# A fused chain of convolutions and Newton inverses on one core: Newton steps as split fp32r products, convolution groups set between them

## The reference

```python
x = x + conv3x3(gn(x), weights) + bias            # A, zero padding
x = x + newton_inverse(gn(x), num_iters=5)        # B
x = x + circular_conv3x3(gn(x), weight)           # C, written as an FFT in the reference
x = x + conv3x3(gn(x), K)                         # D, last row and column of the convolution masked to zero
# gn: 8 groups of 2 channels, mean and variance over the group's 2 x 128 x 128 values
def newton_inverse(W, num_iters):
    scale = max_column_abs_sum(W).max_over_columns * max_row_abs_sum(W).max_over_rows
    X = W.T / scale
    for _ in range(num_iters):
        X = X @ (2 * I - W @ X)
    return X
```

## Time and profile before

| | |
|---|---|
| median of three runs | 698.35 us |
| profiled execution, its own time | 701.13 us |
| its span | 699.5 us |
| TensorE busy (matmuls) | 623.8 us, 89% |
| VectorE busy | 448.1 us, 64% |
| ScalarE busy | 348.9 us, 50% |
| GpSimd busy | 120.7 us, 17% |
| matmuls of V / R / the three convolutions | 168.9 / 137.4 / 303.6 us |
| first Newton step, last Newton product's end | 64.7 us, 641 us |

### The profile page before, as it was taken

The page is one execution under the profiler, slowest core; times in us unless marked ns, Lnnn a source line. Parts: engine busy times, 40 slices in busy tenths (PEclk is TensorE's granted clock), DMA queues, the critical chain, the costliest instruction groups (busy, mean ns, idle before and its releaser), DMA issues.

```text
span 699.5 us, 13159 instructions
## 1 busy us (share of the span) xinstructions
PE 623.8 (89%) x4200; PEld 533.8 (76%) x4200; DVE 448.1 (64%) x1454; ACT 348.9 (50%) x617; POOL 120.7 (17%) x235
## 2 busy tenths in 40 slices
PE   0596894999999999899989999899999999989756
PEld 0365894899879897698869897698879897888544
DVE  3868238766885857766876657856785648356560
ACT  0252552655457265454557374554567265546432
POOL 5024022120213021120212002120210021000202
PEclk9998997999999999999999999999999999999888
DMA  5131043252226314252235314262134214400432
GB/s 153 49 93 42 28 66 114 61 138 58 92 79 146 94 37 126 79 150 60 70 91 128 108 32 133 79 154 62 63 96 99 68 39 131 112 31 32 128 99 60
DMA packets 82837, 60.85 MB, mean 87 GB/s; under 512 B 8238, under 2 KB 75982, under 8 KB 81870
## 3 DMA queue, kind: packets, MB, share of 16 engines
q1 hardware_dynamic: 78558, 54.80, 28.8%
q0 software_dynamic: 4224, 5.43, 3.2%
HBM read 23.46 MB, written 16.91 MB: 58 GB/s over the span
## 4 chain that ended last, share of the span: by engine, by line
PE 69%; DVE 10%; DMA 7%; SPq 6%; issue 5%; ACT 2%; DVEq 0%; POOL 0%; ACTq 0%
PE conv_ps L612 31%; PE V_ps L763 18%; PE R_ps L753 16%; DMA win_C<-rows_dram 4%; SPq L315 3%; DVE x L959 2%; PE R_ps L702 2%; DMA rows_dram<-x 2%; DVE d_A L500 2%; SPq L282 1%; SPq L268 1%; PE V_ps L709 1%; DVE sums L902 1%; DMA x<-out_C 1%; ACT d_C L528 1%
## 5 line engine op out<-in xcount | busy, mean ns | idle before, releaser
L763 PE MATMUL V_ps<-V,R 128*128 128x128 f32 x1280 | 168.9, 276 | 0.0
L763 PEld LDWEIGHTS V_ps<-V,R 128*128 128x128 f32 x1280 | 156.0, 193 | 0.1
L753 PE MATMUL R_ps<-R 128*128 128x128 f32 x1024 | 137.4, 278 | 6.6 <-DVE R L939 6.6
L753 PEld LDWEIGHTS R_ps<-R 128*128 128x128 f32 x1024 | 125.9, 194 | 7.2 <-DVE R L939 7.2
L612 PE MATMUL conv_ps<-d_C,w_C 128*96 128x512 f32 (+1 forms) x486 | 115.7, 393 | 16.4 <-DVE d_C L500 6.4
L612 PEld LDWEIGHTS conv_ps<-d_C,w_C 128*96 128x96 f32 x486 | 76.0, 167 | 48.3 <-DVE d_C L500 11.2
L612 PE MATMUL conv_ps<-d_A,w_D 128*96 128x512 f32 (+1 forms) x432 | 99.6, 386 | 5.5 <-DVE w_D L493 3.9
L830 ACT ACTIVATE R<-R_ps 128x512 f32<-128x512 f32 x128 | 76.0, 594 | 43.0 <-PE R_ps L753 42.3
L832 ACT ACTIVATE V<-V_ps 128x512 f32<-128x512 f32 x128 | 76.3, 596 | 35.6 <-PE V_ps L763 35.6
L612 PE MATMUL conv_ps<-d_A,w_A 128*96 128x512 f32 (+1 forms) x378 | 88.3, 389 | 4.0 <-DVE d_A L500 4.0
L612 PEld LDWEIGHTS conv_ps<-d_A,w_D 128*96 128x96 f32 x432 | 66.8, 164 | 31.1 <-DVE w_D L493 4.0
(11 more groups left out here) (170 smaller groups left out, 644.7 us busy)
## 6 DMA issues: line engine op xcount, KB each, us to landing
win_C<-rows_dram SPq DMA_DIRECT2D x40, 256.0 KB, 4.0
rows_dram<-x SPq DMA_DIRECT2D x32, 256.0 KB
y<-out_D SPq DMA_DIRECT2D x160, 48.0 KB
win_D<-out_C SPq DMA_DIRECT2D x7, 1056.0 KB, 6.8
x<-out_A SPq DMA_DIRECT2D x139, 48.0 KB
win_A<-x SPq DMA_DIRECT2D x84, 64.0 KB
win_A<-x POOLq DMA_DIRECT2D x56, 64.0 KB, 2.8
win_D<-out_C SPq DMA_DIRECT2D x14, 160.0 KB, 5.9
```

Of the source, the lines that this page charges most:

```text
L753: ins = pe.matmul(R_ps[s][:, m, :], Rk[:, m, :], Rk[:, m, :], start=True, stop=True)
L763: ins = pe.matmul(V_ps[s][:, m, :], Rk[:, m, :], V[ch][:, m, :], start=False, stop=True, skip_group_check=True)
```

## The change

The steps are written anew. For each chunk PSUM holds [F | V] side by side, 256 columns a matrix. F starts as -N N^T / s (times a power of two), V as N^T / s with a minus sign; both accumulate over all steps in PSUM, which is never restarted. Between steps ScalarE writes the high part of [F | V] as fp32r, VectorE the low part, and the step multiplies [F | V] by F as high x high, high x low, low x high, 12 fp32r matmuls of 256 columns for four matrices. The last step is plain fp32 and of V alone. A cycle is 24 slots q, strand q % 2, position j = (q // 2) % 6 (0 the start, 1 to 4 split steps, 5 the last), round q // 12. Behind each slot but every fourth stands one convolution group: D of image i - 2 in slots 0 to 7, C of image i - 1 in 8 to 15, A of image i + 2 in 16 to 23. Transposes for the norms and the scale of image i + 1 are made in cycle i.

```diff
+        def pe_slot(pe, b, q):
+            s, r, j = place(q)
+            ch = 2 * r + s
+            if j == 0:
+                pe.wait_ge(s_DS, at(NCHK, b, ch + 1))
+                wait(pe, s_x2, at(NCHK, b, ch - 1 if r else s - 1))
+                for m in range(NMAT):
+                    pe.matmul(z[s][:, m, 128:256], DS[:, c, :], ident, start=m % 2 == 0, stop=True,
+                              is_transpose=True, skip_group_check=True)
+                for m in range(NMAT):
+                    ins = pe.matmul(z[s][:, m, 0:128], DN[:, c, :], DS[:, c, :], start=False, stop=True,
+                                    skip_group_check=True)
+            elif j < STEPS:
+                pe.wait_ge(s_zl[s], at(per_zh, b, (STEPS - 1) * r + j))
+                for m in range(NMAT):
+                    pe.matmul(z[s][:, m, :], zh[s][:, m, 0:128], zh[s][:, m, :], start=False, ...)
+                    pe.matmul(z[s][:, m, :], zh[s][:, m, 0:128], zl[s][:, m, :], start=False, ...)
+                    ins = pe.matmul(z[s][:, m, :], zl[s][:, m, 0:128], zh[s][:, m, :], start=False, ...)
+            else:
+                pe.wait_ge(s_z4[s], at(ROUNDS, b, r + 1))
+                for m in range(NMAT):
+                    ins = pe.matmul(z[s][:, m, 128:256], z4[s][:, m, 0:128], z4[s][:, m, 128:256], ...)
+            ins.then_inc(s_z[s], 1)
...
+        def act_slot(act, b, q):
+            if j == STEPS:
+                return
+            act.wait_ge(s_z[s], at(per_z, b, n_z(r, j)))
+            if j < STEPS - 1:
+                act.activation(zh[s][:, :, :], z[s][:, :, :], ACT.Copy, scale=ROOT[j]).then_inc(s_zh[s], 1)
+            else:
+                act.activation(z4[s][:, :, :], z[s][:, :, :], ACT.Copy, scale=ROOT[j]).then_inc(s_z4[s], 1)
...
+        def dve_slot(dve, b, q):
+            if j < STEPS - 1:
+                dve.wait_ge(s_zh[s], at(per_zh, b, (STEPS - 1) * r + j + 1))
+                dve.scalar_tensor_tensor(zl[s][:, :, :], z[s][:, :, :], ROOT[j], zh[s][:, :, :].bitcast(f32),
+                                         ALU.mult, ALU.subtract).then_inc(s_zl[s], 1)
+            elif j == STEPS:
+                dve_x2(dve, b, 2 * r + s, s, r)
```

TensorE's and VectorE's order around the rows of the next image (cut; each engine's slot stands first or last as shown):

```diff
+        def pe_cycle(pe, i, has_D, has_C, has_A, nxt, load):
+            for q in range(SLOTS):
+                if has_C and q == 3:
+                    row_mean_C(pe, i - 1)
...
+                if nxt and q == 8:
+                    row_mean_B(pe, i + 1)
...
+                pe_slot(pe, i, q)
+                pe_filler(pe, i, q, has_D, has_C, has_A)
...
+        def dve_cycle(dve, i, has_D, has_C, has_A, nxt, load):
+            for q in range(SLOTS):
+                dve_slot(dve, i, q)
+                if has_C and q == 1:
+                    row_stats_1(dve, x2, stC, sC_bn, 1)
...
+                if nxt and q == 5:
+                    dve.wait_ge(s_x1, x1_moved(i + 2))
+                    row_stats_1(dve, x1, stB, sB_bn, 0)
+                if has_C and q == 6:
+                    low_parts(dve, cC, i - 1, 0)
+                if nxt and q == 6:
+                    row_stats_1(dve, x1, stB, sB_bn, 1)
+                if nxt and q == 7:
+                    link_B = dve_rows_B_mean(dve, i + 1)
+                if has_C and q == 7:
+                    low_parts(dve, cC, i - 1, 1)
+                    low_parts(dve, cC, i - 1, 2)
```

SyncE's order. The copy of x1 to x2 is now a DMA, of the whole tensor:

```diff
+        def keep_x1(sp, b):
+            if is_int(b, 0):
+                sp.wait_ge(s_x1, x1_moved(1))
+                sp.wait_ge(s_x1_pool, 16 * n_x1_pool)
+            else:
+                sp.wait_ge(sC_bn, at(2, b, -1))
+            sp.dma_start(x2[:, :, :], x1[:, :, :]).then_inc(s_keep, 16)
...
+        def sp_cycle(sp, i, has_D, has_C, has_A, nxt, load):
+            if has_C:
+                for g in range(NG):
+                    load_x2(sp, i - 1, g)
+            keep_x1(sp, i)
+            if nxt:
+                sp.wait_ge(s_keep, at(16, i, 16))
+                sp.wait_ge(s_DN, at(NCHK, i, NCHK))
+                for g in range(NG):
+                    rows_from_windows(sp, i + 1, g)
+            if has_D:
+                store_y(sp, i - 2)
+            store_x2(sp, i, 0)
+            store_x2(sp, i, 1)
+            if has_C:
+                windows_from_windows(sp, i - 1)
+            if load:
+                for g in range(NG):
+                    load_x(sp, i + 3, g)
+            store_x2(sp, i, 2)
+            store_x2(sp, i, 3)
+            store_x2_edges(sp, i)
```

The low parts of A and D (all but the first two images' A and the last image's D) go to GpSimd, for which ScalarE subtracts the mean from the windows in place in a second activation. GpSimd also forms DS, the scaled DN:

```diff
+        def low_parts_pool(pool, c, b, g):
+            pool.wait_ge(c.s_dh, at(NG, b, g + 1))
+            pool.tensor_tensor(c.d[:, 1, k0:k0 + kn, 1:W + 1], c.win[:, k0:k0 + kn, :],
+                               c.d[:, 0, k0:k0 + kn, 1:W + 1].bitcast(f32), ALU.subtract).then_inc(c.s_dl, 1)
...
+            if low_by_pool(c, b):
+                ins = act.activation(c.win[:, k0:k0 + kn, :], c.win[:, k0:k0 + kn, :], ACT.Identity,
+                                     bias=col(c, NEG))
...
+        def pool_DS(pool, b, ch):
+            if ch == 0:
+                pool.wait_ge(s_sc, at(1, b, 1))
+            pool.tensor_tensor(DS[:, cs, :], DN[:, cs, :], scl[:, 1, cs].unsqueeze(2).broadcast_to([128, NMAT, 128]),
+                               ALU.mult).then_inc(s_DS, 1)
```

More of the change, by code:

```diff
@@ L84, in wait @@
     eng.wait_ge(sem, value)
+KAPPA = [2.0 ** (k - 1) for k in range(STEPS)]
+ROOT = [k ** 0.5 for k in KAPPA]
+SEGS = STEPS + 1
+SLOTS = 2 * ROUNDS * SEGS
 def build(nc, x, w0, b0, w2, w3, consts, y, rows_dram):
@@ L269, in load_x, with rows_from_windows @@
                               x[bass.ds(b, 1), :, lo:hi, :].rearrange("b c h w -> (b h) c w"))\
-                    .then_inc(by_sp if g in SP_X else by_pool, 16)
-        def rows_from_windows(eng, b, g, done=s_x1, first=0):
-            if g == first:
-                wait(eng, s_keep, at(1, b))
-                wait(eng, s_x2, at(NCHK, b - 1, 2))
+                    .then_inc(done, 16)
+        def rows_from_windows(eng, b, g, done=s_x1):
             eng.wait_ge(cA.s_out, at(NG, b, g + 1))
             k0, kn = SPLIT_G[g]
-            out = (cA1 if isinstance(b, int) and b == 1 else cA).out
+            out = (cA1 if is_int(b, 1) else cA).out
             for k in range(k0, k0 + kn):
@@ L696, in pe_gram, with place @@
-        def pe_gram(pe, b, ch):
-            s = ch % 2
-            if ch >= 2:
-                pe.wait_ge(s_R, at(per_R, b, n_R(0, STEPS - 2, s)))
-            for m in range(NMAT):
-                ins = pe.matmul(R_ps[s][:, m, :], DN[:, NMAT * ch + m, :], DN[:, NMAT * ch + m, :],
-                                start=True, stop=True)
-            ins.then_inc(s_Gr, 1)
-        def pe_transposes(pe, out, ch):
+        def place(q):
+            return q % 2, q // (2 * SEGS), (q // 2) % SEGS
@@ L708, in pe_transposes, with pe_norm_T @@
+        def pe_norm_T(pe, b, ch, out=None):
+            pe.wait_ge(s_DN, at(NCHK, b, ch + 1))
+            if out is None:
+                out = spare_ps
+                wait(pe, s_Ta, at(NCHK, b, ch))
             for m in range(NMAT):
@@ new lines, in pe_norm_spread, with pe_filler @@
+        def pe_norm_spread(pe, b):
+            pe.wait_ge(s_dg, at(1, b, 1))
+            pe.matmul(misc_ps[:, M_NB:M_NB + 2 * C], ones_all[0:2 * C, :], diag[:, :],
+                      start=True, stop=True).then_inc(s_nB, 1)
+        def pe_filler(pe, i, q, has_D, has_C, has_A):
+            part, g = filler(q)
+            if part == 0 and has_D:
+                conv_group(pe, cD, i - 2, g, (cA, i + 1) if has_A or not is_int(i, B - 1) else (cC, i - 2))
+            if part == 1 and has_C:
+                conv_group(pe, cC, i - 1, g, (cD, i - 2) if has_D else (cA, i + 1))
+            if part == 2 and has_A:
+                conv_group(pe, cA, i + 2, g, (cC, i - 1) if has_C else (cA, 1))
@@ L777, in pe_cycle @@
                     win_mean(pe, cD, i - 1)
-                if prev and nxt and g == 4:
+                if has_C and q == 23:
                     win_var(pe, cD, i - 1)
-            for k in range(STEPS):
-                pe_step(pe, i, 1, k)
-                if not nxt and k == 0:
-                    win_mean(pe, cD, i - 1)
-                if not nxt and k == 1:
-                    win_var(pe, cD, i - 1)
-                if nxt and k == (3 if prev else 4):
-                    row_mean(pe, sB_bn, sB_sum, i + 1)
@@ new lines, in dve_x2 @@
+        def dve_x2(dve, b, ch, s, r):
+            dve.wait_ge(s_z[s], at(per_z, b, n_z(r, STEPS)))
+            if ch == 0:
+                dve.wait_ge(s_keep, at(16, b, 16))
+            for a in range(NMAT // GC):
+                g = ch * NMAT // GC + a
+                cs = slice(GC * g, GC * (g + 1))
+                ins = dve.scalar_tensor_tensor(x2[:, cs, :], z[s][:, GC * a:GC * (a + 1), 128:256], sx[:, g:g + 1],
+                                               x2[:, cs, :], ALU.mult, ALU.add)
+            ins.then_inc(s_x2, 1)
@@ L1239, in first_convs @@
```

(10 more changed lines are left out.)

816 lines of the change are left out of this document (387 added, 429 removed).

## The result

The changed kernel takes 797.47 us (median of four runs, 795.01 to 802.89) against 697.87 beside it: 1.143 times, 95% interval 1.137 to 1.150. I had forecast slower, 765 us in a range of 715 to 800. The profiled execution took 802.89 us, its span is 801.1.

What follows compares the result with a forecast made beforehand. TensorE was the bound before; now late x1 rows from SyncE's queue stall it 13.7 us a cycle. Five cycles of 87.6, the edge cycles, a 58.5 tail and 8 for the clock gave 765 us, range 715 to 800.

Steps and rivals of the forecast that it cites:

- The stall ahead of slot 8: TensorE idles 13.7 us in every cycle with a next image, waiting on moved x1 rows and their statistics; 76%.
- The copy: SyncE's DMA of x1 to x2 ahead of the row moves: 6.8 us to landing, bounds 3.2 and 7.5.
- VectorE's wait at the rows: Sign that the forecast is right: VectorE waits over 12 us at the row statistics for x1.
- rival 3: Split matmuls take 169 ns each, adding 5 us a cycle behind slot 8: 805 us; 8%.
- rival 1: Moves are bound by data, not issue, so rows land before slot 8: 72.2 us cycles, 652 us, 7% faster; 8%.
- TensorE's price of a split step: Twelve fp32r matmuls of 256 columns at 127 ns: 1.52 us a step, 1.28 to 2.03.
- The lower bound of the low part: VectorE's 128x1024 low part in each split step: 1.27 us, lower bound 1.05 from the slope alone.
- The sums of busy time: Per cycle, VectorE 55 becomes 62 us, ScalarE 43 about 50, GpSimd 13 about 28, all hidden in time summed.
- The clock: Six stalls of over 10 us restart TensorE at a lower clock; half counted, 1.3 us each, 8 in all.
- The edges: Unfilled steps run by latency: slots 16 to 23 take 13.2 us; cycle 6 takes 74.8, cycle 7 59.9.
- VectorE beside GpSimd: VectorE's C low parts and weights wait for GpSimd's SBUF reads: up to 0.8 us on six, 3 a cycle, 789.
- Rival 2: Only part of the stall: rows land at t = 20 to 26 instead of 32.7, 725 to 690 us; 8%.

Runs made afterwards that it cites:

- e5: Changed kernel, but VectorE reads the moved rows after slots 8 and 9 instead of 5 and 6, norms' transposes two slots apart: 736.5 us.
- e6: e5 with the moves on two queues, 12 on SyncE and 10 on GpSimd between its low parts of D: 726.9 us.
- e9: e6 with the split undone: four fp32 matmuls a Newton step, no low part on VectorE: 710.9 us.
- e7: e6 with only high x high multiplied in the split steps, low parts still made: 708.9 us.
- e3: Changed kernel with the low parts of A and D made on VectorE again instead of GpSimd: 800.4 us.
- e4: Changed kernel with only high x high multiplied in the split steps, low parts still made and waited for: 774.4 us.
- e2: Changed kernel, but row statistics read after slots 11 and 12 instead of 5 and 6, norms' transposes in four neighbouring slots: 854.7 us.
- e10: e6 with weights made earlier, A's after slot 13 instead of 15, D's ahead of VectorE's addition to x2 in slot 23: 740.7 us.

## Why the prediction was right, and which terms were off

- **The stall ahead of slot 8: right.** Forecast and measured, in t from the cycle's slot 0: edges landed 2.8 and 3.0, moves from 13.7 and 13.3, VectorE on the rows at 32.7 and 32.4, slot 8 at 37.6 and 36.95; a move 0.79 and 0.80 us. The copy took 5.5 us to its landing (the median of eight) instead of 6.8, but was issued 1.0 later (7.9 instead of 6.9; the terms that I listed for its start add to 7.4, not to the 6.7 that I wrote). TensorE's idle time was 11.05 instead of 13.7, because slots 0 to 7 took 25.9 us, not 23.9. e5 shows that the wait is the cause: it touches no DMA, reads the rows three slots later, and 61 us go. One sign failed: VectorE's wait at the rows was to be over 12 us and was 9.5 to 10.1 in five cycles and 14.1 in one. TensorE's was over 10 in six cycles, as forecast.
- **The number: in part luck.** By itself the stall was to give 740 to 790, and 797.5 lies above that. It lies in 715 to 800 because the range was stretched upwards for half of rival 3, which fell (below). The terms that follow were the ones that filled the gap.
- **What lies under the stall: the step that failed.** Without it I had 72.2 us a cycle and 652 us in all (rival 1). e6 has no wait for rows left in a steady cycle and takes 79.4 a cycle and 727. So the stall was the whole loss in my sum and is 0.091 of the 0.143 in the runs; 0.015 more is the queue (e6), 0.021 the split (e9), and 0.017 stays in what remains of the new order, for which no run here has the cause.
- **TensorE's price of a split step: right in size, wrong in what it was for.** 12 matmuls at 120 ns are 1.44 us (forecast 1.52, bounds 1.28 to 2.03); rival 3 (169 ns) falls. But fp32 steps on [F | V] cost 1.73, not 1.78 (twice the 0.89 of the earlier trace rows), and the 0.29 us saved is bought with VectorE's 1.22 (forecast 1.27) in every step's pass. I had this pass in the sum only for unfilled slots. e6 and e9 have the same steady cycle, though e9's TensorE has 16 x 0.29 us more to do, and e7's is hardly shorter: in filled slots too, waits for VectorE and the lower clock behind them take back what TensorE saves. How much of that is the pass alone no run shows; the waits for low parts are 1.6 us a cycle in e6 and 5.4 in e7. The lower bound of the low part, 1.05, does not come out of the line through the earlier trace rows, whose slope alone gives 1.13; the middle, 1.27, does.
- **The sums of busy time: near.** The three stretches of the cycle above add to 65.3 us for VectorE, 49.0 for ScalarE and 24.8 for GpSimd, where I had 62, 50 and 28.
- **The clock: short by a factor of three.** I counted half a restart for each stall, 1.3 us, 8 in all. The stretches above show 0.50 and 0.82 for 8 us behind the stall, and a second fall to 0.54 behind a wait of only 2.07 us for A's weights; nine matmuls took 3.86 there instead of 2.3. TensorE is busy 76.5 us in this cycle, and its work at full clock was 72.2 in my sum: 4.3 us, an estimate of what the clock cost. From slot 8 on a steady cycle took 55 us instead of 50.0. Over cycles 1 to 5 the steady cycles came out 18 us longer than forecast, before the 8 us allowed for the clock.
- **The edges: too short.** Cycle 0 was 69.6 us instead of 62.5, cycle 6 84.8 instead of 74.8, cycle 7 65.8 instead of 59.9, together 23 us. I priced the slots without convolution groups by the pass alone, 13.2 us for eight; they took 21.8 and 18.3, since TensorE waits there for VectorE's sums for D (3.01 us once, then 1.21 and 1.08) and for its low parts (0.81 each), and the clock falls. The tail added 1.3: 18.3 + 23 + 1.3, 0.3 for a later start, less the 8 for the clock, is the 35 us between the forecast span of 766 and 801.1.
- **VectorE beside GpSimd: no more than before.** The Trainium skill, SBUF — State Buffer (Practical consequences), says that a VectorE instruction with two SBUF inputs contends with a GpSimd one that reads SBUF. From one slow low part in the earlier trace rows I had priced 3 us a cycle for the upper end. The trace agrees with the rule and not with the price: in six cycles one low part of C took 1.53 us instead of 0.75, beside GpSimd's first DN, and one more took 0.92. Of D's the kernel before had one of 1.49 in each of six cycles, so little is new.

```profile
448.12 2.20 DVE L546 SCALAR_TENSOR_TENSOR d_C<-win_C,col_C,d_C 128x512 fp32r<-128x512 f32 x2
448.37 1.41 POOL L1148 TENSOR_TENSOR DN<-x,tB 128x512 f32<-128x512 f32 x1 [2.87 <-DVE devB L624]
```

The copies of the weights were slower in places, 1.18 instead of 0.31 us for D's in three of eight and 0.68 for C's in six of nine. The new low parts of the steps, which read one operand from PSUM, took 1.194 to 1.226 in all 128 cases. e3 has the same six slow low parts of C, but it moves twelve low parts from GpSimd to VectorE, so its time says nothing on the price.

- **Rival 1 (moves bound by data): fell**, 21 moves in 16.77 us again. **Rival 2 (part of the stall)** is what e5 made by hand.

## What to carry to other kernels

When two strands alternate and a new engine enters each step's pass, add up the pass (product, copy, low part, handovers) and not only each engine's sum. Less TensorE work (e4, e7) brought a quarter or less of what it was worth; the rest went into waits for VectorE and into a lower clock. A wait for a DMA queue that stands in the order of an engine on this pass stops TensorE too; reading the result three slots later was worth 61 us and cost no transfer. But moving such a group is safe only if what follows from it keeps its distance: e2 and e10 each took away a wait and made another of the same size, e2 in the norms (75.9 us for 75.7) and e10 at the last x2 (3.7 us for 3.8).
